# Local attention on one core: the scores moved a batch later in the software pipeline, PV ahead of the output projection, and VectorE's division put directly behind PV

## What is computed

```python
h = shift_token(x)
q, k, v = split(h @ wqkv)              # 128 x 1536 per batch
q = l2norm(q) * qs;  k = l2norm(k) * ksc
q, k = rotary_xpos(q, k)
o = local_attention(q, k, v)           # window 64, softmax over 128 keys
x = x + o @ wo
h = layer_norm(shift_token(x)) ...     # then the feed-forward part, groups of 4 batches
```

## Time and profile before

| | us |
|---|---|
| median of 3 runs (1663.01 to 1668.54) | 1665.03 |
| the profiled execution | 1662.99 |
| its span in the profile | 1661.2 |
| TensorE busy in the span | 1483.0 (89%) |
| VectorE, ScalarE, GpSimd busy | 1257.8 (76%), 1112.5 (67%), 892.5 (54%) |
| first to last `d_sq` (L1633) of the two layers | 888.7 to 1559.2 |

### The profile page before, as it was taken

The page is one execution under the profiler, slowest core; times in us unless marked ns, Lnnn a source line. Parts: engine busy times, 40 slices in busy tenths (PEclk is TensorE's granted clock), DMA queues, the critical chain, the costliest instruction groups (busy, mean ns, idle before and its releaser), DMA issues.

```text
span 1661.2 us, 38597 instructions
## 1 busy us (share of the span) xinstructions
PE 1483.0 (89%) x12380; PEld 1229.9 (74%) x12443; DVE 1257.8 (76%) x3064; ACT 1112.5 (67%) x2630; POOL 892.5 (54%) x789
## 2 busy tenths in 40 slices
PE   4888888888878998999986999999888999999888
PEld 3777777677766886777765888888776788888766
DVE  6888888888846557898874788888565677777766
ACT  4877777677735556888773777777532777777632
POOL 5667777677723104555424677777402777777600
PEclk9999999999979998999997999999899999999999
DMA  9700000000012322100000000000000000000000
GB/s 384 304 1 9 9 10 11 8 17 11 10 33 82 87 76 65 36 18 20 16 9 7 15 14 15 13 15 14 8 9 4 9 16 13 15 13 15 9 18 38
DMA packets 75554, 61.30 MB, mean 37 GB/s; under 512 B 40256, under 2 KB 61120, under 8 KB 74688
## 3 DMA queue, kind: packets, MB, share of 16 engines
q1 hardware_dynamic: 71360, 51.69, 9.6%
q0 software_dynamic: 4096, 8.40, 1.7%
HBM read 21.30 MB, written 30.41 MB: 31 GB/s over the span
## 4 chain that ended last, share of the span: by engine, by line
DVE 43%; PE 25%; ACT 18%; issue 9%; POOL 3%; DVEq 1%; DMA 1%; SPq 0%; ACTq 0%; POOLq 0%
ACT d_p L708 10%; DVE slot L1713 5%; DVE d_ss L1696 5%; DVE d_B L1704 4%; DVE d_A L1702 4%; PE slot L459 4%; ACT d_sq L1633 4%; PE slot L460 3%; PE slot L461 3%; PE slot L1832 3%; PE slot L547 3%; DVE c_nm L1377 2%; PE slot L1137 2%; DVE a_mx L728 2%; PE slot L623 2%
## 5 line engine op out<-in xcount | busy, mean ns | idle before, releaser
L1750 POOL TENSOR_TENSOR d_r<-d_vv,nhalf 128x16 f32<-128x16 f32 x64 | 186.1, 2907 | 210.6 <-DVE d_vv L1701 210.6
L993 POOL TENSOR_TENSOR rs<-mv,nhalf 128x1 f32 (+1 forms) x160 | 97.9, 612 | 255.0 <-DVE mv L988 190.1
L708 ACT ACTIVATE d_p<-slot,d_nm,d_r 128x128 f32<-128x128 f32 x512 | 185.6, 468 | 49.3 <-DVE d_nm L1717 49.3
L708 ACT ACTIVATE a_p<-slot,a_nm,a_rq 128x77 f32<-128x77 f32 x512 | 163.8, 429 | 36.0 <-DVE a_nm L732 36.0
L1696 DVE TENSOR_REDUCE d_ss<-d_sq 128x16 f32<-128x1024 f32 x64 | 78.1, 1220 | 99.0 <-ACT d_sq L1633 99.0
L1752 POOL TENSOR_TENSOR d_A<-d_A,d_B 128x1024 f32<-128x1024 f32 x64 | 151.3, 2364 | 0.0
L708 ACT ACTIVATE c_p<-slot,c_nm 128x77 f32<-128x77 f32 x512 | 117.4, 361 | 8.6 <-DVE c_nm L1377 8.3
L1617 PE MATMUL slot<-d_v,d_pT 128*128 128x65 f32 x1024 | 121.4, 272 | 0.0
L1617 PEld LDWEIGHTS slot<-d_v,d_pT 128*128 128x128 f32 x1024 | 119.6, 192 | 0.0
L1347 ACT ACTIVATE c_pT<-slot 77x1024 f32<-77x1024 f32 x64 | 67.0, 1047 | 40.5 <-PE slot L1271 40.4
L1048 POOL TENSOR_TENSOR a_rq<-a_vvq,nhalf 128x16 f32<-128x16 f32 x32 | 93.4, 2918 | 0.0
(11 more groups left out here) (283 smaller groups left out, 4546.2 us busy)
## 6 DMA issues: line engine op xcount, KB each, us to landing
routed<-zero SPq DMA_DIRECT2D x2, 9216.0 KB, 48.9
b_x<-routed SPq DMA_DIRECT2D x80, 64.0 KB, 1.8
answers<-b_y SPq DMA_DIRECT2D x40, 128.0 KB, 1.9
X<-in_x SPq DMA_DIRECT2D x2, 1024.0 KB, 7.3
d_zx<-Z SPq DMA_DIRECT2D x64, 32.0 KB
H<-Z SPq DMA_DIRECT2D x64, 32.0 KB
out<-f_o SPq DMA_DIRECT2D x8, 256.0 KB, 2.0
d_zx<-Z SPq DMA_DIRECT2D x64, 31.8 KB
```

What stands on the lines that cost most here:

```text
L708: i = e.activation(t["p"][:, h, :], R[slot][:, k // nbank, nk * (k % nbank):nk * (k % nbank) + nk], ACT.Exp, bias=t["nm"][:, h:h + 1], sca ...
L993: return e.tensor_tensor(rs[:, bass.ds(b, 1)], mv[:, bass.ds(b, 1), 1:2].rearrange("p a b -> p (a b)"), nhalf[:, 0:1], ALU.pow)
L1750: e.tensor_tensor(t["r"][:, p, :], t["vv"][:, p, :], nhalf[:, 0:16], ALU.pow).then_inc(S("d_key"), 1)
```

## The change

One more lag for the scores and for all behind them, one less for QKV. The lags after it: z transpose and QKV 1, squares and v 1; rotation (A, B, sum of squares) 2; scores and exponentials 4; transposes of p, PV and the division 5; transposes of o, output projection and addition 6; statistics 7. The orders after it:

- TensorE: transposes of A(4), transposes of p(5), z(1), band and scores(4), transposes of o(6), QKV(1), PV(5), output projection(6).
- ScalarE: `d_qT`(4), `d_hTh`(1), `d_pT`(5), `d_oT`(6), exponentials(4), squares(1), v(1).
- VectorE: Z(0), A and B(2), `d_hTl`(1), maximum and `d_nm`(4), sum of squares and `d_vv`(2), statistics(7), division(5), addition(6).
- GpSimd: the addition of A and B now comes ahead of the root `d_r`.

The maximum goes to a corner of R[1] in place of R[0], the output projection to the other bank of R[1], `d_r` has four buffers in place of two, and the hand-made order at the seams moves by a step. No operation is added or taken out. The diff, cut to its core; where lines of the old bodies are only taken out, they are left out here, since the kernel above shows them:

```diff
@@ -306,7 +306,7 @@
...
-d["r"] = at("d_r", [128, 2, 16])
+d["r"] = at("d_r", [128, 4, 16])
...
@@ -1499,16 +1499,14 @@
...
-def qk_slot(it):
-    return R[2] if first_batch(it, 2) else R[0]
+def qk_slot(it, lag):
+    return R[2] if first_batch(it, lag) else R[0]
...
 def v_bank(it):
-    return R[3][:, 1, :] if first_batch(it, 2) else R[1][:, 0, :]
+    return R[3][:, 1, :] if first_batch(it, 1) else R[1][:, 0, :]
...
 def z_bank(it):
-    if first_batch(it, 1, 1):
-        return R[2 + it.i - 1][:, 0, 128:256]
-    return R[1][:, 0, 128:256]
+    return R[2][:, 0, 128:256] if first_batch(it, 1) else R[1][:, 1, 128:256]
...
@@ -1532,54 +1530,34 @@
...
+        b = it.b(4)
...
+            if it.seen(5):
+                e.wait_ge(S("d_exp"), it.upto(5, B))
             e.wait_ge(S("d_key"), count(b, 3, 3, base=B))
...
+        b = it.b(5)
...
+            if it.seen(6):
+                e.wait_ge(S("d_div"), nth(it.upto(6, B), 2, 2))
             e.wait_ge(S("d_exp"), count(b, base=B))
...
+                mm = e.transpose(R[3][:, c // 4, 128 * (c % 4):128 * (c % 4) + 128], t["p"][:, it.m(5, 2), c, :], ident[:])
...
+        b = it.b(1)
...
+            if it.seen(7):
+                e.wait_ge(S("d_add"), it.upto(7, B))
+            e.wait_ge(S(f"d_z_{it.m(1, 4)}"), 8 * (b + B) + 32 - 8 * it.m(1, 4))
+            e.transpose(z_bank(it), t["z"][:, it.m(1, 4), :], ident[:]).then_inc(S("d_zT"), 1)
+        b = it.b(4)
...
             e.wait_ge(S("d_qkT"), count(b, base=B))
...
@@ -1590,93 +1568,95 @@
...
+        b = it.b(6)
...
+            if it.seen(7):
+                e.wait_ge(S("d_add"), it.upto(7, B))
+            if it.seen(1):
+                e.wait_ge(S("d_hl"), it.upto(1, B))
+            e.wait_ge(S("d_div"), count(b, 2, 2, base=B))
...
+                mm = e.transpose(R[1][:, 1, 128 * c:128 * c + 128], t["on"][:, it.m(6, 2), 128 * c:128 * c + 128], ident[:])
+            mm.then_inc(S("d_OT"), 1)
         b = it.b(1)
...
+            elif past(b - 1):
+                e.wait_ge(S("d_rot"), count(b - 1, 1, 3, base=B))
+            e.wait_ge(S("d_hl"), count(b, base=B))
...
+                mm = passes(e, qk_slot(it, 1)[:, h, :], x, [w[:, 512 * h:512 * h + 512] for w in wqkv[l]])
+            mm.then_inc(S("d_qkp"), 1)
...
+            elif not first_batch(it, 2):
+                e.wait_ge(S("d_v"), count(b - 1, base=B))
+            if it.seen(4):
+                e.wait_ge(S("d_max"), nth(it.upto(4, B), 2, 2))
+            passes(e, v_bank(it), x, [w[:, 1024:1536] for w in wqkv[l]]).then_inc(S("d_vp"), 1)
         b = it.b(5)
...
+        b = it.b(6)
...
+            e.wait_ge(S("d_oTe"), count(b, base=B))
...
+                mm = e.matmul(R[1][:, 1, 0:128], t["oT"][:, c, :], wol[:, l, c, :], start=(c == 0), stop=(c == 3))
+            mm.then_inc(S("d_wo"), 1)
...
 def da_scalar(e, l):
...
+        b = it.b(4)
...
+            e.wait_ge(S("d_qkTp"), count(b, base=B))
+            e.activation(t["qT"][:].rearrange("p (a c) t -> p a (c t)", a=2), R[2][:], ACT.Copy).then_inc(S("d_qkT"), 1)
+        b = it.b(1)
...
+            e.wait_ge(S("d_zT"), count(b, base=B))
+            e.activation(t["hT"][0][:, it.m(1, 2), :], z_bank(it), ACT.Copy).then_inc(S("d_hh"), 1)
+        b = it.b(5)
...
+            e.wait_ge(S("d_PT"), count(b, base=B))
+            e.activation(t["pT"][:].rearrange("p (a c) t -> p a (c t)", a=2), R[3][:], ACT.Copy).then_inc(S("d_pT"), 1)
+        b = it.b(6)
...
+            e.wait_ge(S("d_OT"), count(b, base=B))
+            e.activation(t["oT"][:].rearrange("p c t -> p (c t)"), R[1][:, 1, :], ACT.Copy).then_inc(S("d_oTe"), 1)
+        b = it.b(4)
...
+            e.wait_ge(S("d_max"), count(b, 2, 2, base=B))
...
+            exponentials(e, {"p": t["p"][:, it.m(4, 2), :, :], "nm": t["nm"]}, 2, 0, 4, 128, S("d_exp"),
...
+        b = it.b(1)
...
             e.wait_ge(S("d_qkp"), count(b, base=B))
...
+                e.wait_ge(S("d_rot"), count(b - 1, 2, 3, base=B))
...
+            e.activation(t["sq"][:].rearrange("p (a b) -> p a b", a=2), qk_slot(it, 1)[:], ACT.Square).then_inc(S("d_sq"), 1)
             e.wait_ge(S("d_vp"), count(b, base=B))
...
+            if past(b - 4):
+                e.wait_ge(S("d_PV"), count(b - 4, base=B))
...
 def da_vector(e, l):
...
+        p = it.m(2, 2)
...
@@ -1687,54 +1667,64 @@
...
         b = it.b(2)
...
+            e.wait_ge(S("d_sq"), count(b, base=B))
+            if past(it.i - 4):
+                e.wait_ge(S("d_qkTp"), count(it.i - 4, base=B))
...
         b = it.b(1)
...
             e.wait_ge(S("d_hh"), count(b, base=B))
...
+        b = it.b(4)
...
+            e.wait_ge(S("d_S"), count(b, base=B))
+            if it.seen(2):
+                e.wait_ge(S("d_v"), it.upto(2, B))
+            e.tensor_reduce(R[1][:, 0, 0:8], R[2][:].rearrange("p a (j k) -> p a j k", k=128), AX.X, ALU.max, negate=True)\
+                .then_inc(S("d_max"), 1)
...
+            e.wait_ge(S("d_max"), count(b, 1, 2, base=B))
+            e.tensor_tensor(t["nm"][:].rearrange("p (a j) -> p a j", a=2), R[1][:, 0, 0:8].rearrange("p (a j) -> p a j", a=2),
+                            t["r"][:, it.m(4, 4), 0:8].rearrange("p (j a) -> p a j", a=2), ALU.mult).then_inc(S("d_max"), 1)
+        b = it.b(2)
...
+            e.tensor_reduce(t["ss"][:, p, :], t["sq"][:].rearrange("p (h d) -> p h d", d=DL), AX.X, ALU.add)\
+                .then_inc(S("d_rot"), 1)
+            e.wait_ge(S("d_rot"), count(b, 2, 3, base=B))
+            if past(it.i - 4):
+                e.wait_ge(S("d_key"), count(it.i - 4, 2, 3, base=B))
+            e.tensor_scalar(t["vv"][:, p, :], t["ss"][:, p, :], 1e-24, None, ALU.max).then_inc(S("d_rot"), 1)
+        b = it.b(7)
...
+            e.wait_ge(S(f"d_h2_{m}"), 8 * (b + B) + 32 - 8 * m)
...
+            e.bn_stats(st[:, 0, :], rows(H2, b)).then_inc(S("ac_bn"), 1)
...
+        b = it.b(5)
...
+            e.wait_ge(S("d_PV"), count(b, base=B))
+            e.reciprocal(rc, o[:, :, :, 64]).then_inc(S("d_div"), 1)
+            e.wait_ge(S("d_div"), count(b, 1, 2, base=B))
+            e.tensor_tensor(t["on"][:, it.m(5, 2), :].rearrange("p (a j k) -> p a j k", a=2, j=4), o[:, :, :, 0:64],
+                            rc.unsqueeze(3).to_broadcast([128, 2, 4, 64]), ALU.mult).then_inc(S("d_div"), 1)
+        b = it.b(6)
...
+            e.wait_ge(S("d_wo"), count(b, base=B))
+            e.tensor_tensor(rows(Z, b), rows(Z, b), R[1][:, 1:2, 0:128], ALU.add).then_inc(S("d_add"), 1)
...
 def da_pool(e, l):
@@ -1744,17 +1734,17 @@
         b = it.b(2)
         if b is not None:
             p = it.m(2, 2)
-            e.wait_ge(S("d_rot"), count(b, 2, 3, base=B))
-            if past(it.i - 4):
-                e.wait_ge(S("d_exp"), count(it.i - 4, base=B))
-            e.tensor_tensor(t["r"][:, p, :], t["vv"][:, p, :], nhalf[:, 0:16], ALU.pow).then_inc(S("d_key"), 1)
+            e.wait_ge(S("d_rot"), count(b, 1, 3, base=B))
+            e.tensor_tensor(t["A"][:, p, :], t["A"][:, p, :], t["B"][:, p, :], ALU.add).then_inc(S("d_key"), 1)
             e.wait_ge(S("d_rot"), count(b, 3, 3, base=B))
-            e.tensor_tensor(t["A"][:, p, :], t["A"][:, p, :], t["B"][:, p, :], ALU.add).then_inc(S("d_key"), 1)
+            if past(b - 4):
+                e.wait_ge(S("d_exp"), count(b - 4, base=B))
+            e.tensor_tensor(t["r"][:, it.m(2, 4), :], t["vv"][:, p, :], nhalf[:, 0:16], ALU.pow).then_inc(S("d_key"), 1)
             e.wait_ge(S("d_key"), count(b, 2, 3, base=B))
             A = t["A"][:, p, 512:1024].rearrange("p (h d) -> p h d", d=DL)
-            e.tensor_tensor(A, A, t["r"][:, p, 8:16].unsqueeze(2).to_broadcast([128, HL, DL]), ALU.mult)\
+            e.tensor_tensor(A, A, t["r"][:, it.m(2, 4), 8:16].unsqueeze(2).to_broadcast([128, HL, DL]), ALU.mult)\
                 .then_inc(S("d_key"), 1)
-        b = it.b(6)
+        b = it.b(7)
         if b is not None:
             e.wait_ge(S("ac_ve"), count(b, base=B + 2 * NB))
             root(e, b).then_inc(S("ac_rs"), 1)
@@ -1767,8 +1757,8 @@
...
-        if it.static and l > 0 and it.i in (0, 4, 5):
-            e.wait_ge(S("f_add"), count((0, 1, NG - 1)[(0, 4, 5).index(it.i)]))
+        if it.static and l > 0 and it.i in (0, 4, 6):
+            e.wait_ge(S("f_add"), count((0, 1, NG - 1)[(0, 4, 6).index(it.i)]))
...
         if b is not None:
...
@@ -1780,9 +1770,9 @@
                 apart(e)
...
-        b = it.b(5)
-        if b is not None:
-            s = S(f"d_h2_{it.m(5, 4)}")
+        b = it.b(6)
+        if b is not None:
+            s = S(f"d_h2_{it.m(6, 4)}")
             e.wait_ge(S("d_add"), count(b, base=B))
...
@@ -1807,6 +1797,7 @@
                 elif c == 1:
                     e.wait_ge(S("d_div"), count(last, 2, 2))
                 else:
+                    e.wait_ge(S("d_v"), count(last))
                     e.wait_ge(S("d_oTe"), count(last))
                     e.wait_ge(S("d_add"), count(last))
             if b is not None:
@@ -1823,7 +1814,6 @@
```

(39 more changed lines are left out.)

146 lines of the change are left out of this document (28 added, 118 removed).

## The result

The changed kernel took 1674.76 us in the median of 4 runs against 1664.28 (ratio 1.0049, interval 1.0025 to 1.0072), and in a second series 1673.89 against 1667.57 (1.0031, 1.0017 to 1.0044; one execution of its 14, at 3842 us, is left out). The forecast was 1658.0, range 1642 to 1672.

A forecast was written before the change was run, and what follows sets the result against it. A ScalarE and VectorE loop was taken to bound the step at 9.23 us, TensorE close under it. Stretches -10.2 and -7.5, seams +8 and +4, ends -1 gave -6.7 from 1663.0; forecast median 1658, range 1642 to 1672.

The forecast's parts named there:

- Layer 1: Steady step bound by TensorE at 9.14 us in place of 9.23; first transposes of A to last of p 290.4 us.
- The loop over ScalarE and VectorE: Exponentials, squares, A, B, maximum and exponentials again, 9.23 us a step; cut by the change, 8.4 us left with hand-overs.
- the step that failed: Layer 0's steady step: `d_hTl` ends at 3.8 us, just when the transposes of o need it; at most 0.1 us more.
- the forecast of the stretch: First transposes of A to last of p: 290.4 us in each layer, 10.2 less in layer 0, 7.5 in layer 1.
- rival 1: Nothing gained: `d_hTl` late at the transposes of o or costlier operand changes; step 9.23 to 9.3, 1663 to 1666; chance 0.27.
- Rival 4: GpSimd's root blocks VectorE's `mv`; steps 10.1 us in layer 0, 9.6 in layer 1, total 1696; chance 0.10.
- Rivals 2 and 3: TensorE has more room, step 8.8 us, total 1640, chance 0.08; TensorE stays at half clock into full steps, 1671, 0.10.
- The seams: Longer start ahead of the first transposes of A: +8 us in layer 0 (5 to 11), +4 in layer 1 (2 to 7).
- The layers' ends: The last but one output projection no longer waits for its `d_oT` ahead of PV: -0.5 us each, -1 in all.
- The rule weighed: TensorE headroom read from weight loads, 83% busy: step could fall to 7.7, exponentials' loop of 8.4 binds, near 1618 us.

The follow-up runs named there:

- e6: The changed kernel with a needless normalisation like Z put first in VectorE's step in layer 1; that layer's step took 9.18 us, from 9.06.
- e13: The changed kernel with GpSimd's product on the keys waiting, in layer 0, for VectorE's Z of the same step; 1664.17 us, 0.9997 of the kernel before.
- e5: The changed kernel run and profiled once more, unchanged; 1673.89 us, ratio 1.0031 to the kernel before.

## Why the prediction was wrong

- **Layer 1: right, by its mechanism and its size.** The terms by the timeline of the step at 1410.67, start to start: transposes of A to band 2.16 (forecast 2.16), band to the transposes of o and these 2.04 (2.12), QKV 2.17 (2.18), PV 1.73 (1.80), output projection 0.95 (0.90): 9.05 against 9.14. The loop over ScalarE and VectorE was cut, and TensorE is the bound. The stretch of 289.9 us had a mean granted clock of 1.00; in the other profiles with this code in layer 1 it took 289.7 to 292.1.
- **Layer 0: the step that failed** is "A is free for VectorE when the transposes end, 1.04; A, B and `d_hTl` [...] end at 3.8". VectorE is not free then: it is in Z until 1.8 us behind the first transpose of A (1109.71 against 1107.95), held by the product. `d_hTl` ends at 4.3 in place of 3.8. The prediction itself put the root's end at 9.8, so the product at 0.7 to 1.7 of the next step, and the addition's end at 9.6 with Z behind it, at 0.5; it never laid the two side by side. By those numbers Z would have led by 0.2 us, and by e6 that is enough; measured, both start at 0.6. So the missing piece was not only the pair but how little separated them. That cost 0.46 a step against layer 1, and 10.5 us against the forecast of the stretch. `d_hTl` late was named as rival 1, with the right sign to look for, but as a general risk of 0.1 us.
- **That step was not all.** With it repaired (e13) the kernel is level with the one before, not 6.7 us faster: layer 0 takes 292.5 us for the 290.4 forecast, layer 1 291.9, and the layers' ends cost 2.1 where 1.0 was to be gained. The part ahead of the first z transpose, 6.7 us more in the profiled execution, was in no term of the sum and is open (e5).
- **The trace of before had it.** Its timeline, one step of VectorE and GpSimd:

```profile
1097.36 2.36 POOL L1752 TENSOR_TENSOR d_A<-d_A,d_B 128x1024 f32<-128x1024 f32 x1
...
1098.27 0.29 DVE L1725 BATCH_NORM_STATS2 st<-H 128x6 f32 x1 [0.15 <-issue]
...
1098.87 0.17 DVE L986 BATCH_NORM_AGGREGATE agg<-st 128x2 f32<-128x6 f32 x1
1099.18 0.55 DVE L988 TENSOR_TENSOR mv<-agg,eps 128x2 f32 x1
...
1099.80 1.04 POOL L1755 TENSOR_TENSOR d_A<-d_A,d_r 128x512 f32<-128x512 f32 x1
...
1100.50 0.42 DVE L1686 TENSOR_SCALAR Z<-X,mv,rs  x1
```

  Z took 0.42 in place of its free 0.34 and ended 0.08 behind the product. A hold of 0.08 us looks like nothing. It was the tail of one that can last as long as the product, and the change slid Z into it from the front. Three steps at the layer's start already showed more: 0.59 and 0.60 behind the addition, 1.02 behind the product. The same rows hold a second pair: `mv`, 0.16 us when free, took 0.49 to 0.72 in all 27 steps from 932 to 1173 and ended with the addition.
- **Rival 4: the right resource, the wrong pair.** `mv` took 0.16 us inside a root of 2.92 (above), so this root did not hold it. What holds is GpSimd's product and addition, and what is held is Z, and before the change `mv`. The row on `mv` in the earlier trace rows was the addition's work, and so pointed at the pair to look for. The change moved `mv` out of the addition and so freed it, and moved Z wholly into the product.
- **Rivals 2 and 3: no.** Layer 1's step was 9.06, not 8.8, with the wait for `d_qT` in it. From the first transposes of A to the last of p the granted clock was 0.99 and 1.00 of full in the two layers, against 0.98 and 0.99 before, so no time was lost to it there.
- **The seams: right in size** (+6.2 in the bounds 5 to 11, +4.9 in 2 to 7).
- **The layers' ends: wrong by sign, small.** Not -0.5 each but +1.0 and +0.6. At layer 0's end the chain goes through the addition's rows on their way to H and on to the statistics, which now come a lag later; that this is the reason was not tested:

```profile
1217.37 0.53 SPq L1777
...
1217.94 3.40 DMA H<-Z
...
1221.48 0.30 DVE st L1713
```

- **The rule weighed**, that of the Trainium skill, "Perfetto Trace Analysis", section on identifying the most-contended engine, to read headroom from the weight loads: it does not agree with this case. Layer 1's weight loads are busy 218.34 of 260 us (84%, from 1325 to 1585) after the change, the chain goes through TensorE, and no kernel run here has a step under 9.05. The starts in the rows were the better guide.

## What to carry to other kernels

Before moving work, lay out one step of every engine on one time axis and look for pairs on VectorE and GpSimd. If a VectorE instruction takes longer than when it is alone and ends each time at the same small distance behind a GpSimd one (here 0.08 us for Z, 0.02 for `mv`), it is held, however small the loss is now. When slack is taken out of a schedule, holds that it had covered come due. Where two instructions must not meet, order them by a semaphore rather than by luck: a start 0.1 us earlier or later, or a loop turn, otherwise decides. And count a steady step's gain against the seams: here 14 us in the layers bought a longer start of each, and little was left.
